# Two gated layers on one Trainium2 core: sums of four states side by side, convolution on TensorE, work in other slots

## The reference, cut to what matters

```python
x_ssm, gate = split(xn @ W_in + b_in, 2)                 # 128 channels each
x_conv = silu(causal_conv(x_ssm, conv_w, 4 taps) + conv_b)   # per channel, along the tokens
B, C = split(x_conv @ W_x + b_x, 2)                      # 16 states each
h = A[None] * h + xc_t[:, :, None] * B_t[:, None, :]     # for each token; h is (128 channels, 16 states)
y = einsum('bn,bdn->bd', C_t, h) + D_param * xc_t
y = (y * silu(gate)) @ W_out + b_out
```

## Time and profile before

| | |
|---|---|
| device time, median of 3 runs | 659.96 us (655.25 to 660.21) |
| the profiled execution: time, span | 660.97 us, 659.2 us |
| granted TensorE clock, mean | 0.954 |
| busy: PE, DVE, POOL, ACT | 80%, 74%, 54%, 49% of the span |
| chain that ended last: PE, DVE, issue, ACT, POOL | 40%, 29%, 14%, 11%, 3% |
| scans of unit 0 begin; of unit 7 end | 129.1 us; 649.8 us |

### The profile page before, as it was taken

How to read it: one execution, slowest core, us unless ns; L and a number is a source line. 1 busy time by engine, 2 the same in 40 slices (tenths; PEclk the granted TensorE clock), 3 DMA queues, 4 the chain that set the end, 5 groups by cost and what they waited for, 6 DMA issues and landing times.

```text
span 659.2 us, 6095 instructions
## 1 busy us (share of the span) xinstructions
PE 530.5 (80%) x1795; PEld 311.9 (47%) x1795; DVE 487.5 (74%) x751; ACT 323.8 (49%) x546; POOL 353.9 (54%) x316
## 2 busy tenths in 40 slices
PE   1358887798988998798898988889889888777774
PEld 0235655465645664465455654656456433323331
DVE  2520230477889898977968998878699969998965
ACT  3336586567644655376535843566545632432110
POOL 1724453388438673755647764684376635433333
PEclk9998998999998999998999999899999988879969
DMA  8200000000000000000000000000000000000000
GB/s 327 84 2 0 18 0 1 16 0 1 0 17 0 33 0 16 2 32 1 16 1 30 3 0 0 9 25 0 0 1 16 1 0 0 16 1 0 16 0 16
DMA packets 5505, 11.63 MB, mean 18 GB/s; under 512 B 736, under 2 KB 1504, under 8 KB 5216
## 3 DMA queue, kind: packets, MB, share of 16 engines
q1 hardware_dynamic: 4464, 9.47, 4.0%
q10 hardware_dynamic: 1008, 1.77, 0.8%
HBM read 9.13 MB, written 2.10 MB: 17 GB/s over the span
## 4 chain that ended last, share of the span: by engine, by line
PE 40%; DVE 29%; issue 14%; ACT 11%; POOL 3%; DMA 1%; DVEq 0%; SPq 0%; POOLq 0%; ACTq 0%
PE bank0a L796 13%; PE ybank L902 6%; DVE hs L1151 6%; DVE xbank L1138 6%; PE bank1a L878 4%; PE bank1a L852 3%; DVE plain L1041 2%; ACT plain L530 2%; PE xbank L894 2%; DMA Bt<-w_in 1%; ACT L518 1%; DVE beats L1115 1%; PE bank0a L754 1%; POOL hidAl L445 1%; DVE beats L1113 1%
## 5 line engine op out<-in xcount | busy, mean ns | idle before, releaser
L457 POOL TENSOR_TENSOR pr<-hs,Ct 128x512 f32<-128x512 f32 x128 | 174.1, 1361 | 145.7 <-DVE hs L1151 134.2
L902 PE MATMUL ybank<-pr,gat 128*128 128x512 f32 x256 | 136.9, 618 | 5.7 <-POOL pr L457 5.7
L894 PE MATMUL xbank<-xpair,spr 128*128 128x512 f32 x128 | 97.3, 760 | 17.0 <-DVE hs L1151 16.9
L1138 DVE TENSOR_TENSOR xbank<-xbank,Bt 128x512 f32<-128x512 f32 x128 | 88.2, 689 | 28.9 <-PE xbank L894 28.7
L445 POOL TENSOR_TENSOR hidAl<-plain,hidAh 128x512 fp32r<-128x512 f32 x48 | 63.1, 1316 | 62.2 <-ACT hidAh L531 52.3
L445 POOL TENSOR_TENSOR hidBl<-plain,hidBh 128x512 fp32r<-128x512 f32 x48 | 62.6, 1307 | 48.9 <-ACT hidBh L531 45.7
L1151 DVE TENSOR_TENSOR_SCAN hs<-decay,carry,xbank 128x512 f32<-128x512 f32 x64 | 81.7, 1277 | 7.4 <-DVE xbank L1138 0.5
L1151 DVE TENSOR_TENSOR_SCAN hs<-decay,xbank 128x512 f32<-128x512 f32 x64 | 77.8, 1215 | 6.3
L902 PEld LDWEIGHTS ybank<-pr,gat 128*128 128x128 f32 x256 | 48.0, 196 | 40.3 <-issue 20.9
L796 PE MATMUL bank0a<-hidAh,hTh 128*128 128x512 f32 x128 | 56.7, 443 | 8.4 <-ACT hidBh L531 7.2
L796 PE MATMUL bank0a<-hidBh,hTh 128*128 128x512 f32 x128 | 58.0, 453 | 1.8 <-ACT hidAh L531 1.6
(11 more groups left out here) (150 smaller groups left out, 1035.6 us busy)
## 6 DMA issues: line engine op xcount, KB each, us to landing
xt<-x_tok SPq DMA_DIRECT2D x8, 256.0 KB, 2.8
xr<-x_feat SPq DMA_DIRECT2D x8, 256.0 KB, 8.1
out<-xr SPq DMA_DIRECT2D x8, 256.0 KB, 2.0
fh<-h_w SPq DMA_DIRECT2D x1, 1024.0 KB, 11.2
pr<-h_w SPq DMA_DIRECT2D x1, 1024.0 KB, 13.8
lw<-l_w ACTq DMA_DIRECT2D x1, 640.0 KB, 7.2
g<-spread ACTq DMA_DIRECT2D x1, 512.0 KB, 6.3
Bt<-w_in SPq DMA_DIRECT2D x1, 512.0 KB, 9.0
```

The source lines that it names most:

```text
L457: pool.tensor_tensor(pr[:, i % NPR, :], hs[:, i % NHS, :], Ct[:, hs_(u)], ALU.mult).then_inc(p_ready, 1)
L894: pe.matmul(xbank[i % 2][:], spr[:, at, :], xpair[:, half, hs_(u)], start=True, stop=True).then_inc(xs_full, 1)
L902: pe.matmul(ybank[:], gat[:, P - DPG * (k + 1):2 * P - DPG * (k + 1)], pr[:, i % NPR, :], start=(k == 0), stop=(k == NGRP - 1)).then_inc(y ...
L1138: dve.tensor_tensor(xbank[i % 2][:], xbank[i % 2][:], Bt[:, hs_(u)], ALU.mult).then_inc(xb_ready, 1)
```

## The change

- **Sums of states.** The states have 8 buffers `hs` and no `pr`: POOL multiplies by C in place. Slot k works on group `group_of(k)`, so that four successive slots hold groups 0, 4, 8, 12 (then 1, 5, 9, 13, ...), one for each 32 rows of the output. PE sums four at once, in slots 4, 8, 12 and slot 0 of the next period: four products with 32 columns of weights each, to rows 0-31, 32-63, 64-95, 96-127 of `ybank`. A scan waits for the sum of eight steps before. POOL copies the carried column of even units before it multiplies.
- **Convolution.** The weights of the projection are multiplied by each tap once, by POOL, at the start (`w_conv`, from a new 256 KB array `conv_rows`). PE adds four fp32 products with shifted inputs into `bank1a` in slots 7 and 8, with short products for the first three tokens (the end of the unit before, or a correction of the bias at the start of a sequence). DVE forms the biases once (7 small orders). `take_ssm` and the four DVE orders a unit are gone; ACT reads silu from `bank1a` in slot 9, the gate follows in slot 10.
- **Slots.** Compares of even units stand in slots 9, 10, 12, 13, 13, 13, 14, 14 (were 10, 11, 11, 12, 13, 13, 14, 14), of odd units in 6, 6, 7, 7, 8, 9, 10, 12 (were 7, 7, 10, 11, 11, 12, 13, 13), with 3 buffers `beats` for 4. `score` moves to slot 6, `score_column` to 7 and 8, its copies to 8 and 9; `mod_down` of `last` from 1 to 2, `mod_update` from 2 to 3, the gate's silu (`mod_gate`) from 3 to 4; `low_x` from 12 to 11.

```diff
-NHS = 3
-NPR = 4
-NBEATS = 4
+NSTATES = 8
+QUAD = 4
+NBEATS = 3
+def group_of(k):
+    return k % QUAD * (NGRP // QUAD) + k // QUAD
...
-    return (7, 7, 10, 11, 11, 12, 13, 13) if u % 2 else (10, 11, 11, 12, 13, 13, 14, 14)
+    return (6, 6, 7, 7, 8, 9, 10, 12) if u % 2 else (9, 10, 12, 13, 13, 13, 14, 14)
...
@@ pool: weigh_states
+                h = hs[:, i % NSTATES, :]
...
-                if i >= NPR:
-                    pool.wait_ge(y_full, i - NPR + 1)
                 pool.wait_ge(xs_done, i + 1)
-                pool.tensor_tensor(pr[:, i % NPR, :], hs[:, i % NHS, :], Ct[:, hs_(u)], ALU.mult).then_inc(p_ready, 1)
+                if u % 2 == 0:
+                    pool.tensor_copy(carry[:, k:k + 1], h[:, HALF - 1:HALF]).then_inc(carried, 1)
+                    pool.wait_ge(carried, u // 2 * NGRP + k + 1)
+                pool.tensor_tensor(h, h, Ct[:, hs_(u)], ALU.mult).then_inc(p_ready, 1)
@@ act: convolved
-                act.activation(xc[:, hs_(t)], cv[(TAPS - 1) % 2][:, hs_(t)], ACT.Silu, bias=scale("conv_b")).then_inc(xc_ready, 1)
+                take1(("conv", t), xc[:, hs_(t)], ACT.Silu, bias=b_conv[:, 0:1])
@@ pe: convolve, in slot 7 with (3, 2) and in slot 8 with (1, 0)
+                    for k in taps:
+                        s = TAPS - 1 - k
+                        if s > 0 and t % 2 == 1:
+                            pe.matmul(bank1a[:, 0:s], w_conv[:, k, :], ynT[:, (t - 1) % NYNT, HALF - s:HALF],
+                                      start=False, stop=False)
+                        last = pe.matmul(bank1a[:, s:HALF], w_conv[:, k, :], ynT[:, t % NYNT, 0:HALF - s],
+                                         start=(s == 0), stop=(k == 0))
+                        if s == 0 and t % 2 == 0:
+                            pe.matmul(bank1a[:, 0:TAPS - 1], ident[:], b_edge[:], start=False, stop=False)
@@ pe: gather_y, in slots 4, 8, 12 and 0 of the next period, at the end of the slot
-                pe.wait_ge(p_ready, i + 1)
-                pe.matmul(ybank[:], gat[:, P - DPG * (k + 1):2 * P - DPG * (k + 1)], pr[:, i % NPR, :],
-                          start=(k == 0), stop=(k == NGRP - 1)).then_inc(y_full, 1)
+                pe.wait_ge(p_ready, step(u, QUAD * (quad + 1)))
+                at = P // QUAD - DPG * (quad + 1)
+                for j in range(QUAD):
+                    rows = slice(j * P // QUAD, (j + 1) * P // QUAD)
+                    pe.matmul(ybank[rows, :], gat[:, at:at + P // QUAD], hs[:, step(u, QUAD * quad + j) % NSTATES, :],
+                              start=(quad == 0), stop=(quad == NGRP // QUAD - 1)).then_inc(y_full, 1)
@@ dve: scan
-                if i >= NHS:
-                    dve.wait_ge(p_ready, i - NHS + 1)
...
+                if i >= NSTATES:
+                    dve.wait_ge(y_full, i - NSTATES + 1)
```

More of the change, by code:

```diff
@@ L118 @@
     if _n is not None:
-        L1_ACT += [(_k, _n) for _k in ("xnT", "ssm", "score", "gate", "B", "C")]
+        L1_ACT += [(_k, _n) for _k in ("xnT", "score", "conv", "gate", "B", "C")]
     if _u is not None:
@@ L137, in done, with program @@
     return order.index(job) + 1
-def program(nc, x_tok, x_feat, small, w_in0, h_w, w3T, retention_w, l1_w, w2_l1, decay_mask, gamma_row,
+def program(nc, x_tok, x_feat, small, w_in0, h_w, w3T, retention_w, l1_w, w2_l1, conv_rows, decay_mask, gamma_row,
             identity, before_mask, spread, gather, out):
@@ L497, in _ @@
             act.dma_start(grow[:], gamma_row).then_inc(params, 16)
-            for dst, src in ((raw_spr, spread), (lw[:], l1_w), (gat[:], gather), (tri[:], before_mask), (w2l[:], w2_l1)):
+            for dst, src in ((raw_spr, spread), (lw[:], l1_w), (gat[:], gather), (tri[:], before_mask), (w2l[:], w2_l1),
+                             (gate[:, 0:TAPS * P], conv_rows)):
                 act.dma_start(dst, src).then_inc(l1_params, 16)
@@ L604, in take_gate, with convolved @@
             def take_gate(t):
+                take1(("gate", t), gate[:, hs_(t)], ACT.Silu, bias=scale("b_in", 1))
+            def convolved(t):
+                if t == 0:
+                    act.wait_ge(b_conv_step, 5)
+                    act.wait_ge(w_conv_ready, 1)
                 if t >= 2:
                     act.wait_ge(yg_ready, t - 1)
[L607 to L613, removed]
+                take1(("conv", t), xc[:, hs_(t)], ACT.Silu, bias=b_conv[:, 0:1])
+                act.wait_ge(l1_act_done, done(L1_ACT, ("conv", t)))
                 for half in range(2):
@@ L619, in take_B @@
             def take_B(t):
+                if t >= 2:
+                    act.wait_ge(xs_done, step(t - 1, 0))
                 take1(("B", t), Bt[:, hs_(t)], ACT.Identity, bias=scale("b_x", 0))
@@ L633, in mod_gate @@
                 act.activation(g1[:, hs_(t)], g1[:, hs_(t)], ACT.Silu).then_inc(g1_ready, 1)
[L635 to L639, removed]
             def slot(p, k):
                 last, u, n, v, w = units(p)
[L643 to L646, removed]
                 if v is not None and 1 <= k < 1 + KT:
                     z_round(v, k - 1)
-                if last is not None and last != UNITS - 1 and k == 3:
+                if last is not None and last != UNITS - 1 and k == 4:
                     mod_gate(last)
@@ L924, in slot @@
                         elif k == 6:
-                            project("ssm", n, W_IN[:, 0:P])
+                            project("score", n, W_R)
                         elif k == 7:
-                            project("score", n, W_R)
-                    if last is not None and last != UNITS - 1 and k == 1:
+                            convolve(n, (3, 2))
+                        elif k == 8:
+                            convolve(n, (1, 0))
+                    if last is not None and last != UNITS - 1 and k == 2:
                         mod_down(last)
@@ L936, in slot @@
                         project_out(last)
-                    if u is not None and u % 2 == 0 and 8 <= k < 10:
-                        score_column(u + k - 8)
+                    if u is not None and u % 2 == 0 and 7 <= k < 9:
+                        score_column(u + k - 7)
                     if w is not None:
@@ L969, in slot @@
                         value(v)
-                    if u is not None and k > 0:
-                        gather_y(u, k - 1)
+                    if u is not None and k > 0 and k % QUAD == 0:
+                        gather_y(u, k // QUAD - 1)
                     elif last is not None and k == 0:
-                        gather_y(last, NGRP - 1)
+                        gather_y(last, NGRP // QUAD - 1)
                 for p in PERIODS:
@@ L1177, in slot @@
                     stats_l1(n)
-                if n is not None and 8 <= k < 10:
-                    convolve(n, 2 * (k - 8))
                 if u is not None:
@@ L1183, in slot @@
                     gate_y(last)
-                if last is not None and last != UNITS - 1 and k == 2:
+                if last is not None and last != UNITS - 1 and k == 3:
                     mod_update(last)
@@ L1201, in slot @@
                         mod_update(u)
-                if n is not None and k == 12:
+                if n is not None and k == 11:
                     low_x(n)
```

97 lines of the change are left out of this document (51 added, 46 removed).

## The result

| | before | after |
|---|---|---|
| device time, median of 20 runs each | 658.1 us | 661.0 us |
| ratio, with its 95% interval | | 1.0049 [1.0027, 1.0071] |
| profiled execution: time, span | 660.97, 659.2 us | 663.07, 661.3 us |
| granted TensorE clock, mean | 0.954 | 0.905 |
| scans of unit 0 begin | 129.1 us | 130.7 us |

The clock in the tables of runs is that of the profiled execution.

The account below looks back on a forecast made before the run. Four stages a period with different limits: DVE, PE, PE and ACT in turn, mostly PE. Three pairs -4.8, unit 6 -2, unit 7 +1.3, period -1 +1: -4.5 from 660.97, 656.5; median forecast 655 us, own range -8 to +10, rivals 637 to 676.

Parts of the forecast that it names:

- G: Time of four 32-column sums side by side on PE: taken as 2.14 us, bounds 0.86 and 3.44.
- stage C: Slots 9 to 13, q to first `mod_up`, PE and ACT in turn: as many ACT links as before, 0 us.
- third rival: Odd units, slot 7: DVE waits up to 3.8 us for a compare buffer; if not hidden 665 us, chance 0.13.
- full overlap: Rival: all four sums of a group run together in 0.86 us, giving 638 us, some 637 with unit 6; chance 0.20.
- The start: Start-up before the units: more loads, one POOL order and seven small DVE orders, 0 us, bound +1.
- Lower clock: PE idles more; if all periods became like even ones (0.95), another 5 us; widens the forecast, no chance of its own.
- Stage A: Slots 0 to 3, limited by DVE: odd periods gain 0, even -1.4 us; `mod_down` in slot 2 lies beside DVE's chain.
- Stage B: Slots 4 to 8, PE without a gap: odd periods +2.8 us, even +0.1 with the wait for scores gone.
- Stage D: Slots 14 and 15, mostly PE: -2.2 us in odd periods, -0.9 in even ones.
- The convolution: PE, slots 7 and 8: four products for one projection, +2.58 us; short products +0.2 odd, +0.7 even.
- Unit 6: Its period is DVE's: 4.07 us less there, but the convolution on PE delays the next spread: -2, bounds -4 and +1.
- Tail: Unit 7, after the last scan: PE's one sum becomes a group, +1.3 us.

Follow-up runs that it names:

- e15: Changed kernel with the gate's projection in slot 10 instead of 9 and 4 compare buffers instead of 3, no zero products: 642.4 us, ratio 0.9773 to before.
- e1: Changed kernel with only PE's gate projection moved from slot 9 to slot 10: 655.4 us, ratio 0.9946 to before.
- e12: Changed kernel with only the compare buffers raised from 3 to 4: 657.3 us, ratio 0.9989 to before.
- e4: Changed kernel with a group's four sums as full 128-column products, one after the other: 691.7 us, ratio 1.0487 to before.
- e7: Changed kernel with eight fp32r products of zeros on PE in slot 9, ahead of the gate's projection: 655.0 us, ratio 0.9940 to before.
- e3: Changed kernel with the gate's projection in slot 10 and mod_down, mod_update, mod_gate back in slots 1, 2, 3: 663.1 us, ratio 1.0067 to before.
- e6: Kernel before with only the convolution moved to PE, sums of one state a slot: 678.4 us, ratio 1.0295 to before.
- e2: Changed kernel with only mod_down, mod_update and mod_gate back in slots 1, 2, 3: 662.9 us, ratio 1.0058 to before.

## Why the prediction was wrong

I forecast -4.5 us with G = 2.14; it came out at +3.2, slower by more than the measurement's doubt, though within 1%. Two errors of opposite sign lie behind the small number.

**The step that failed: stage C, priced at 0.** I wrote that "the chain of ACT passes has as many links as before". The count is right and the question was wrong. Before, the taps ran on DVE, `bank1a` was free when the gate's projection came, and no wait of that projection for ACT stands in the trace. Now the bank holds the convolution until ACT reads it, and ACT reads it behind q's pass and a table load of 1.28 us: 13.7 us of PE waits in six periods. From q to the first `mod_up`, stage C grew by 0.1, 2.8, 1.2, 1.5 and 2.4 us in units 0 to 4 (8.1 in all, the table above), and e15 brings it below the kernel before. Together with it failed the weight of my third rival, the **compare buffers**. Its place (slot 7 of odd units), its length (I said up to 3.8 us, it is 2.97) and its releaser were right, and I let DVE's slack hide it because DVE was busy only 59 of 70 us: a share of a period, where the waits lie in single slots. The wait for the bank isn't in the prediction at all, so I could not see that the two bind in turn; e1, e12 and e15 show that mending both is worth more than the parts. Both mended, the kernel runs 18.2 us faster than as changed.

**The size that was off the other way: G.** I let the second record of a pair hold up the next pair (2.14 us). It doesn't: eight records end in 0.99 us, and the next spread takes 0.2 us more, 1.19 in all. Thirteen groups at 0.95 us less make my sum -4.5 - 12.4 = -16.9 us. So the **full overlap** rival (G of 0.86) had the right mechanism and the wrong time, 638 us, since it kept the 0 of stage C. The Trainium skill's "TensorEngine Tiling (Array Packing)", "Theoretical Speedup", gives up to 4x for 32 columns; the trace has 3.43 / 0.99 = 3.5 for the group alone and 3.66 / 1.42 = 2.6 with the spread behind it. The rule in its "Key Properties", that a change of tiling mode drains TensorE, fits the 0.2 us behind each group, in size four times the estimate that I drew from those pages for one change and twice the estimate for two. In e4, whose groups have as many increments of semaphores and no narrow products, the 0.2 us is absent; what in the switch costs it no run shows.

The two together: -16.9 + 18.2 = +1.3 for a measured +3.2, or in other words e15 at -14.9 us where the sum with the right G and a free stage C says -16.9. The start came 1.6 us later than before, where I had 0 with a bound of +1, which would bring the sum to +2.9; but the same start ends between 129.4 us (e7) and 132.3 us (e4) in other executions, so 1.6 us can't be counted on. The closeness is in part luck, since the clock also moved: e15 has 0.924, not 0.954.

**Lower clock** I named and gave no case of its own. It fell further than its "all like the even ones" (0.95): to 0.86 in unit 1's period and 0.80 in unit 6's. In unit 1's, the chain of waits has the third and fourth `mod_up` at the lower level, 1.2 GHz, where unit 3's take 1.14 and 1.13:

```profile
259.79 2.09 PE bank1a L897 x2
...
262.64 2.08 PE bank1a L897 x2
```

That the clock has a part in the loss is shown by the zeros, which do no work and win 7.2 us in the gate's slot alone. With both waits mended, zeros bring only 3, so most of that part goes with the waits; which period runs at the lower clock differs from kernel to kernel (unit 1's after, 0.86; units 3's and 5's in e3, 0.88), and no run settles why.

The other steps:
- *Stage A*: odd 0, even -1.4. `z_product` 3 of unit 3 comes 16.1 us after the period's start, 16.0 before; the even period reaches its first h1 product 1.5 us sooner. Right. But `mod_down` didn't "lie beside DVE's chain": it begins behind a wait of 1.9 us, at the lower clock, and the chain above runs through it (4.44 us) into `mod_update` and `z_product` 3. It replaced one wait by another of the same end.
- *Stage B*, odd: in PE's order of time 359.02 to 375.81, 16.8 us against 15.4, +1.4. My terms with G = 1.19 give 2.8 - 1.9 = +0.9. What I left out: four ranks of the moved compares lie in this stage instead of two (+0.4). A short product costs 0.12 us and the shifted one behind it 0.96 for 0.86, together the 0.22 that I had. I counted the ranks only where they left (stage D), not where they arrived.
- *Stage B*, even: 17.2 us against 18.7 in unit 2, -1.5; my terms with that G give 0.1 - 1.9 = -1.8, of which -0.9 is q's own length and -0.9 the way to its start. The wait for the scores is gone, as said, and q took 1.10 us for 1.92.
- *Stage D*, from the second `mod_up` to the period's end: -2.1 in unit 3 (said -2.2), -1.4 in unit 2 (said -0.9). Right for these; in unit 1, with two `mod_up` at the lower clock, it grew by 1.0.
- *The convolution*: +19 us alone (e6); my terms for its products come to some 20 (2.8 in each of three odd periods, 3.3 in each of three even ones, and 1 to 2.8 in period -1). But e6 also holds 14.0 us of waits for the bank, against 4.1 us a unit less work for DVE, so that the two are close is no check. That the sums of four pay for it rests on e4.
- *Unit 6*: 52.0 us for 55.5 (first product with B to the next unit's), said -2 with a bound of -4. *Tail*: the last group starts with a lowered clock and takes 2.06 us, said 2.14 for another reason.

## What to carry to other kernels

When an operation moves from one engine to another, ask who now owns the buffer between them and for how long: a PSUM bank read by a queue that also loads a table is a wait, however few the links. Count a moved compare, and its rank product, where it arrives too; and weigh a wait against the slack of the slots around it, not of the period. Two waits that bind in turn look small one by one: try both mends together before dropping either.

## What the runs showed of the hardware

- Four fp32 products of 128x512 with 32 columns of weights each, to four different quarters of the output rows, take 0.99 us together; one of 128 columns takes 0.86, four of them 3.43. The two records of each product don't hold up the next one's: one behind the other by pairs they would need 2.14.
- The first full-width product behind such a group takes 0.43 us in the chain instead of 0.23: about 0.2 us per group.
- An fp32 product with one to three columns of data costs 0.12 us in the chain of waits, and the product of 509 to 511 columns behind it 0.96 instead of 0.86. Unit 2, one column:

```profile
297.59 0.86 PE bank1a L866 x2
298.45 0.12 PE bank1a L864 x2
298.56 0.96 PE bank1a L866 x2
```

- Relieving PE lowered its clock: 0.954 before, 0.904 with only the sums of four, 0.905 after, 0.947 with the groups at full width, 0.970 with only the convolution added.
- A product behind a wait of 2.69 us took anything from 1.13 to 2.07 us: 1.13, 2.07, 1.38, 2.07, 1.94 in units 0 to 4 of the kernel after, and 1.12 or 1.13 in all five of e2.
